# Second feed-forward of a two-layer block: hidden state kept transposed, mean square applied to the result

## The chip, the cores and the metric

The kernel runs on one core of a Trainium2 chip. The metric is the device time of one execution in microseconds (us), as a median over runs. One execution was also recorded by the hardware profiler; durations below come from it.

## What is computed

Two transformer layers over x, 2 sequences of 1024 rows of 256 numbers. Layer 0 is layer norm, causal attention (32 query heads, 8 key heads of 8) and beside it a GELU feed-forward in fp8. Layer 1 is layer norm, an attention among the 16 heads of 16 at each of the rows of a tile, and beside it the feed-forward that this change touches:

```
wq_gu = ternary_quant(w_gate_up)
gu = jnp.einsum('bsd,hd->bsh', x, wq_gu)
gate, up = jnp.split(gu, 2, axis=-1)
h = jax.nn.silu(gate) * up
hn = rms_norm(h)          # h / sqrt(mean(h*h) + eps), over the 1024 hidden units
wq_p = ternary_quant(w_proj)
return jnp.einsum('bsh,dh->bsd', hn, wq_p)
```

The result of each layer is added to x.

## The kernel before

The rows are cut in 16 tiles of 128. Every engine runs one fixed list of steps, the table `ORDER`: a step is a name and a number, `gu.63` or `qk.80`, and `run[name](n)` issues its instructions. The lists hold the steps of all stages of all tiles mixed; they set the order on each engine, and semaphores (`w.wait_ge`) hold a step back until its inputs and buffers are there. Nothing is reordered at run time between the matmuls of TensorE or on the other engines.

Layer 0's attention is 144 quads. A quad is four score matmuls (`qk`, L674) into the four banks `psS`, two exponentials on ScalarE (`exp`, L922) into `Pt`, and four f32 matmuls (`pv`, L688) into `psV`. All other matmuls fill the three shared PSUM banks `psM` (psA, psB, psC) in turn; a step may fill a bank only when the step three fills back has been read out.

The second feed-forward, tile n, with its steps:

- `xn1Tc` and `xl` make the normed tile, transposed (features on partitions), as a high and a low f16 part, `xhs`.
- `gu`, four steps a tile (TensorE, L837): `xhs` is the stationary operand, 512 columns of the ternary weights `wguT` stream. Four matmuls fill a bank with rows on partitions and 512 hidden units on the free axis.
- `tg` (ScalarE, tanh), `sg`, `hh` (VectorE): silu(gate) times up into `h1`, 128x1024 f32.
- `ssq` (ScalarE, L986): square with a running sum into `ss`; `ssm` (VectorE, L1402) and `rsg` (GpSimd, L1618) make 1/sqrt(mean + eps) of each row.
- `hxa` (ScalarE, L991) and `hx` (VectorE, L1408): `h1` times that factor, as a high and a low f16 part `hx_b`.
- `hxT`, two steps (TensorE, L847), eight transposes each; `hTc`, two steps (VectorE, L1416), copy them to SBUF as `hT`.
- `dn1` (TensorE, L856): 16 matmuls, `hT` stationary, 256 columns of `wpT` stream.
- `yo` adds the attention's result (from `at1T`, `wo1`), `yout` (VectorE, L1438) adds `dn1`'s, `ysum` sums absolute values for a check of range, and `out` stores the tile.

After the last tile a check (`rng`, `out_of_range`, L1444 to L1471) decides whether a second, safer pass has to run; it isn't run for these inputs. `h1`, `hx_b` and `hT` are single buffers, so `hh` of a tile waits for `hx` of the tile before it, and `hTc` for its `dn1`.

## Time and profile before

| what | value |
|---|---|
| median of 3 runs | 611.24 us (610.84 to 611.49) |
| the profiled execution, whole | 610.33 us |
| its span, first to last instruction | 608.6 us |
| mean granted TensorE clock | 0.988 |
| TensorE matmul busy | 559.7 us, 92% of the span |
| ScalarE busy | 468.5 us, 77% |
| VectorE busy | 445.6 us, 73% |
| GpSimd busy | 257.9 us, 42% |
| chain that ended last, by engine | PE 66%, DVE 13%, ACT 9%, issue 6%, DMA 2%, POOL 1% |

PE is TensorE, PEld its weight loads, DVE is VectorE, ACT ScalarE, POOL GpSimd. A matmul's recorded duration holds its way through the array, and consecutive ones overlap; what one costs the engine is the distance from its start to the start of the next. An f32 matmul with an f32 stationary operand is recorded as two.

### The profile page before, as it was taken

To read this page: it belongs to the slowest core of one execution; us is meant where nothing else is said; L and a number is where in the kernel's file an instruction comes from. 1 tells how busy PE (TensorE), PEld (TensorE's weight loads), DVE (VectorE), ACT (ScalarE), POOL (GpSimd) and SP (SyncE) were. 2 spreads that over 40 slices of the span, in tenths; PEclk is the share of its full clock that TensorE was granted. 3 is DMA by queue.
4 is the path that set the end of the run, shared out by engine and by line. 5 is a ranking of instruction groups with operands and counts; after the bars stand their busy time and mean duration, and the time that the engine had idled before them with its cause. 6 is when DMAs were issued, how large, how long until landed. Compare 5 with 4: busy or idle time off the path is not lost.

```text
span 608.6 us, 13144 instructions
## 1 busy us (share of the span) xinstructions
PE 559.7 (92%) x5040; PEld 290.9 (48%) x5085; DVE 445.6 (73%) x903; ACT 468.5 (77%) x605; POOL 257.9 (42%) x318
## 2 busy tenths in 40 slices
...
DMA packets 150915, 30.40 MB, mean 50 GB/s; under 512 B 133952, under 2 KB 149568, under 8 KB 150848
## 3 DMA queue, kind: packets, MB, share of 16 engines
...
q14 instruction: 26, 0.21, 0.1%
...
## 4 chain that ended last, share of the span: by engine, by line
PE 66%; DVE 13%; ACT 9%; issue 6%; DMA 2%; POOL 1%; SPq 0%; DVEq 0%; ACTq 0%; POOLq 0%
PE psV L688 16%; PE psS L674 7%; ACT Pt L922 5%; PE psA L837 3%; PE psS L791 3%; PE psC L837 2%; PE psB L837 2%; DMA stage<-in_wg 1%; PE psA L725 1%; PE psA L856 1%; PE psC L753 1%; PE psB L753 1%; PE psC L754 1%; DVE ga L1276 1%; DMA x<-in_x 1%
## 5 line engine op out<-in xcount | busy, mean ns | idle before, releaser
L922 ACT ACTIVATE Pt<-psS 128x1024 f32<-128x1024 f32 x288 | 280.5, 1036 | 45.7 <-PE psS L674 25.7
L688 PE MATMUL psV<-Pt,vaug 128*32 128x512 f32 x1152 | 147.1, 602 | 1.5 <-POOL Pt L1563 1.2
L1563 POOL TENSOR_SCALAR_AFFINE_SELECT Pt<-Pt 128x1024 f32<-128x1024 f32 x64 | 74.5, 1188 | 41.7 <-ACT Pt L922 41.5
L674 PE MATMUL psS<-qTf,kTf 32*128 32x512 f16 x576 | 72.4, 386 | 5.0 <-DVE qTf L1184 2.5
L674 PEld LDWEIGHTS psS<-qTf,kTf 32*128 32x128 f16 x576 | 19.5, 91 | 82.7 <-ACT Pt L922 45.1
L688 PEld LDWEIGHTS psV<-Pt,vaug 128*32 128x32 f32 x1152 | 26.1, 108 | 47.3 <-issue 37.6
L1618 POOL TENSOR_TENSOR ss<-ss,mhalf 128x1 f32<-128x1 f32 x16 | 9.8, 613 | 83.6 <-DVE ss L1402 83.5
L971 ACT ACTIVATE stage<-psS 128x1024 f32<-128x1024 f32 x32 | 31.1, 1025 | 12.5 <-PE psS L791 12.4
L1543 POOL TENSOR_TENSOR rt<-qkv,cs 128x320 f32<-128x320 f32 x16 | 17.0, 1059 | 50.0 <-DVE qkv L1138 47.1
L1554 POOL TENSOR_TENSOR QXf<-rt,QXf 128x512 f16<-128x512 f32 x16 | 21.4, 1339 | 35.3 <-ACT QXf L909 35.1
L1609 POOL TENSOR_TENSOR r<-qk,cos 128x256 f32<-128x256 f32 x16 | 13.0, 810 | 43.5 <-ACT qk L955 43.5
L1276 DVE SCALAR_TENSOR_TENSOR ga<-gw,gb 128x512 bf16<-128x512 f32 x32 | 29.1, 910 | 1.6 <-ACT gw L948 1.6
L1267 DVE SCALAR_TENSOR_TENSOR gw<-gw,gb 128x512 f32<-128x512 f32 x32 | 26.1, 815 | 1.7 <-ACT gw L937 1.7
L1408 DVE SCALAR_TENSOR_TENSOR qtmp<-qtmp,ss 128x1024 f16<-128x1024 f32 x16 | 21.5, 1345 | 5.8 <-ACT qtmp L991 5.7
L1599 POOL TENSOR_TENSOR xhs<-xn1T,xhs 128x256 f16<-128x256 f32 x16 | 12.2, 761 | 30.3 <-DVE xhs L1319 30.3
L1279 DVE TENSOR_TENSOR ga<-ga,fb 128x512 bf16<-128x512 bf16 x32 | 21.2, 663 | 3.7 <-ACT fb L943 0.5
L1546 POOL TENSOR_TENSOR rt<-qkv,sn 128x160 f32<-128x160 f32 x32 | 23.4, 751 | 0.0
L986 ACT ACTIVATE qtmp<-qtmp 128x1024 bf16<-128x1024 f32 x16 | 17.0, 1063 | 8.1 <-issue 5.1
L948 ACT ACTIVATE gw<-gw 128x512 f32<-128x512 f32 x32 | 20.8, 649 | 2.3 <-DVE gw L1267 2.2
L837 PE MATMUL psB<-wguT,xhs 128*128 128x512 bf16 x77 | 20.5, 379 | 2.0 <-issue 1.4
L837 PE MATMUL psA<-wguT,xhs 128*128 128x512 bf16 x75 | 19.8, 379 | 2.2 <-issue 1.0
L1283 DVE CAST a<-ga 128x512 fp8e4<-128x512 bf16 x32 | 20.9, 654 | 1.1
...
## 6 DMA issues: line engine op xcount, KB each, us to landing
...
```

The lines of the kernel that those rows point to most:

```text
L674: e.matmul(psS[j], kd[32 * j:32 * j + k, h, 128 * at:128 * at + 128], qd[32 * j:32 * j + k, 4 * h:4 * h + 4, :].rearrange("p s n -> p (s n ...
L688: ins = e.matmul(psV[32 * j:32 * j + 32, :], vaug[:, at, j, 32 * h:32 * h + 32], Pt[(4 * Q + j) % NP], start=(kb == 0 and h == 0), stop=(k ...
L837: ins = e.matmul(bank[:], src[:, pt, 128 * c:128 * c + 128], wguT[:, c, c0:c0 + 512], start=(k == 0), stop=(k == 3))
L922: e.activation(flat(Pt4[:, u % NP:u % NP + 2, :]), flat(psS4[:, j:j + 2, :]), ACT.Exp, scale=scale).then_inc(S["exp"], 1)
L971: e.activation(P1[:, 4 * b:4 * b + 8, :].rearrange("p g n -> p (g n)"), flat(psS4[:, b:b + 2, :]), ACT.Exp, scale=SC1).then_inc(S["ex1"], 1)
L1267: e.scalar_tensor_tensor(gw[:, half, :], gw[:, half, :], 1.0 / GA, gb[:, half, :], ALU.add, ALU.mult).then_inc(S["ge1"], 1)
L1276: e.scalar_tensor_tensor(a, gw[:, half, :], 1.0, gg, ALU.add, ALU.mult).then_inc(S["ge3"], 1)
L1279: e.tensor_tensor(a, a, fb[:, half, :], ALU.mult).then_inc(S["ge3"], 1)
L1408: e.scalar_tensor_tensor(hx_b[:, 1, :], h1, sn[:, 2:3], hx_b[:, 0, :], ALU.mult, ALU.subtract).then_inc(S["hx"], 1)
L1546: e.tensor_tensor(rb[:, :, :, ev], pairs[:, :, :, 1 - ev], snv[:, :, ev].unsqueeze(1).to_broadcast([128, 40, 4]), ALU.mult).then_inc(S["ro ...
L1554: e.tensor_tensor(X4[:, 0:32, 2:4, :], heads(rt[n % len(rt)][:, 0, 0:256], 2), X4[:, 0:32, 0:2, :], ALU.subtract).then_inc(S["ql"], 1)
L1563: e.affine_select(out=p, in_=p, pattern=[[0, 8], [1, 128]], compare_op=ALU.is_ge, fill=0.0, base=0, channel_multiplier=-1).then_inc(S["mas ...
```

## The change

The hidden state is made with hidden units on partitions. `gu` swaps its operands: 128 columns of the weights are stationary and the 128 columns of `xhs` stream, so that a bank holds four blocks of 128 hidden units by 128 rows. `h1` is then already what `dn1` needs as stationary operand, so `hxT` and `hTc` go. A row's sum of squares now lies across partitions: `ssq` writes the squares to `hsq`, `hsr` adds the eight blocks in one VectorE reduction (read with a stride of 128), and one more f32 matmul behind the 16 of `dn1`, against a column of ones, adds over the partitions into column 256 of the same bank. `msq` (VectorE) and `rsh` (GpSimd) make the factor, and `yout` multiplies `dn1`'s result with it. `hxa` and `hx` no longer wait for the factor. The check takes in the mean squares (`rngb`).

```diff
     "pe": (
-        "xnT.0 qkv.0 xnT.1 ts.0 ts.1 xnT.2 qkv.1 qxT.0 qxT.1 xnT.3 td.0 qk.0 td.1 tr.0 up.0 tr.1 qkv.2 qk.1 ts.2 "
...
+        "xnT.0 xnT.1 ts.0 ts.1 qkv.0 qkv.1 xnT.2 td.0 td.1 tr.0 qxT.0 tr.1 qxT.1 xnT.3 ts.2 qk.0 qk.1 qkv.2 pv.0 "
...
                 bank = shared("gu", m)
                 for k in range(4):
-                    c, pt = k % 2, k // 2
-                    c0 = 1024 * o + 512 * half
-                    ins = e.matmul(bank[:], src[:, pt, 128 * c:128 * c + 128], wguT[:, c, c0:c0 + 512], start=(k == 0),
-                                   stop=(k == 3))
+                    c0 = 1024 * o + 512 * half + 128 * k
+                    for i in range(4):
+                        c, pt = i % 2, i // 2
+                        ins = e.matmul(bank[:, 128 * k:128 * k + 128], wguT[:, c, c0:c0 + 128],
+                                       src[:, pt, 128 * c:128 * c + 128], start=(i == 0), stop=(i == 3))
                 ins.then_inc(S["gu"], 1)
-            def hxT(m):
...
-                for s in range(8):
-                    ins = e.transpose(bank[:, s, :], hx_b[:, pt, 128 * s:128 * s + 128], identh[:])
...
             def dn1(n):
-                w.wait_ge("hTc", 2 * n + 2)
+                w.wait_ge("hxa", n + 1)
+                w.wait_ge("hx", n + 1)
                 w.wait_ge("tw", 12)
                 bank = shared("dn1", n)
                 for k in range(16):
                     pt, s = divmod(k, 8)
-                    ins = e.matmul(bank[:, 0:256], hT[:, pt, s, :], wpT[:, s, :], start=(k == 0), stop=(k == 15))
+                    ins = e.matmul(bank[:, 0:256], hx_b[:, pt, 128 * s:128 * s + 128], wpT[:, s, :], start=(k == 0),
+                                   stop=(k == 15))
+                if n < NT:
+                    w.wait_ge("gz", 3)
+                    w.wait_ge("hsr", n + 1)
+                    ins = e.matmul(bank[:, 256:257], hsum, onesf[:, 0:1], start=True, stop=True)
                 ins.then_inc(S["dn1"], 1)
...
             def ssq(n):
                 w.wait_ge("hh", 2 * n + 2)
-                w.wait_ge("hxT", 2 * n)
-                w.wait_ge("hx", n)
-                e.activation(hx_b[:, 0, :].bitcast(BF16), h1, ACT.Square,
-                             accum_out=ss[n % len(ss)][:, 0:1]).then_inc(S["ssq"], 1)
+                w.wait_ge("hsr", n)
+                w.wait_ge("hnm", n - NT)
+                e.activation(hsq, h1, ACT.Square).then_inc(S["ssq"], 1)
 
             def hxa(n):
-                w.wait_ge("rsg", n + 1)
-                e.activation(hx_b[:, 0, :], h1, ACT.Copy, scale=ss[n % len(ss)][:, 2:3]).then_inc(S["hxa"], 1)
+                w.wait_ge("hh", 2 * n + 2)
+                w.wait_ge("hnm", n - NT + 1)
+                w.wait_ge("dn1", n)
+                e.activation(hx_b[:, 0, :], h1, ACT.Copy).then_inc(S["hxa"], 1)
...
+                w.wait_ge("ssq", n)
+                e.scalar_tensor_tensor(h1[:, 512 * half:512 * half + 512], sg1, 0.5 * UH if n < NT else 0.5, bank[:],
+                                       ALU.mult, ALU.mult).then_inc(S["hh"], 1)
...
+            def hsr(n):
+                w.wait_ge("sin", 1)
                 w.wait_ge("ssq", n + 1)
-                e.tensor_scalar(sn[:, 1:2], sn[:, 0:1], 1.0 / 1024, F32EPS, ALU.mult, ALU.add).then_inc(S["ssm"], 1)
+                w.wait_ge("dn1", n)
+                e.tensor_reduce(hsum, hsq.rearrange("p (s n) -> p n s", n=128), AX.X, ALU.add).then_inc(S["hsr"], 1)
...
             def hx(n):
-                sn = ss[n % len(ss)]
                 w.wait_ge("hxa", n + 1)
-                w.wait_ge("hxT", 2 * n)
-                e.scalar_tensor_tensor(hx_b[:, 1, :], h1, sn[:, 2:3], hx_b[:, 0, :], ALU.mult,
-                                       ALU.subtract).then_inc(S["hx"], 1)
-
-            def hTc(m):
-                n, pt = divmod(m, 2)
-                bank = psM[filled["hxT", m] % len(psM)][:].bitcast(F16).rearrange("p (s n) -> p s n", n=128)
-                w.wait_ge("hxT", m + 1)
                 w.wait_ge("dn1", n)
-                e.tensor_copy(hT[:, pt, :, :], bank).then_inc(S["hTc"], 1)
+                e.tensor_tensor(hx_b[:, 1, :], h1, hx_b[:, 0, :], ALU.subtract).then_inc(S["hx"], 1)
...
+            def msq(n):
+                bank = psM[filled["dn1", n] % len(psM)]
+                w.wait_ge("dn1", n + 1)
+                e.tensor_scalar(msqs[:, n:n + 1], bank[:, 256:257], 1.0 / 1024, F32EPS * UH * UH, ALU.mult,
+                                ALU.add).then_inc(S["msq"], 1)
...
+                if n < NT:
+                    w.wait_ge("rsh", n + 1)
+                    e.scalar_tensor_tensor(dst[:], bank[:, 0:256], ss[n % len(ss)][:], yo_b[n % len(yo_b)][:], ALU.mult,
+                                           ALU.add).then_inc(S["yout"], 1)
+                else:
+                    e.tensor_tensor(dst[:], bank[:, 0:256], yo_b[n % len(yo_b)][:], ALU.add).then_inc(S["yout"], 1)
...
+            def rsh(n):
+                w.wait_ge("msq", n + 1)
+                w.wait_ge("yout", n + 1 - len(ss))
+                e.tensor_tensor(ss[n % len(ss)][:], msqs[:, n:n + 1], mhalf[:], ALU.pow).then_inc(S["rsh"], 1)
```

All five lists of `ORDER` are written anew, in a different mix; TensorE's goes from 788 steps to 756, the 32 `hxT` fewer. Two places of them follow, as rows of instructions (line, operation, output<-streamed operand, stationary operand, size, count).

The first is TensorE's end of the program, before: from `dn1.13` (L856 into psB) over `gu.63` (L837) and the transposes of tile 14 (L847) to the first ones of tile 15.

```order
L856 MATMUL psB<-wpT,stmp 128x256 x16
L837 MATMUL psC<-wguT,xhs_1 128x512 x4
L847 MATMUL psA<-identh,qtmp 128x128 x8
L847 MATMUL psB<-identh,qtmp 128x128 x8
L579 MATMUL psC<-identf,at1_0 128x128
L580 MATMUL psC<-identf,at1_0 128x128
L823 MATMUL psA<-wo1,at1T_0 128x256
L824 MATMUL psA<-wo1,at1T_0 128x256
L856 MATMUL psB<-wpT,stmp 128x256 x16
L579 MATMUL psC<-identf,at1_0 128x128
L580 MATMUL psC<-identf,at1_0 128x128
L847 MATMUL psA<-identh,qtmp 128x128 x8
```

There follow `hxT.31`, `wo1.15` and `dn1.15`. The same engine in the change, from `gu.63` (now L843) to its last step but the check: L860 and L865 are `dn1` with its new last matmul, L828 and L829 `wo1`.

```order
L843 MATMUL psC<-xhs_1,wguT 128x128 x16
L860 MATMUL psA<-wpT,qtmp 128x256 x16
L865 MATMUL psA<-onesf,ang 128x1
L828 MATMUL psB<-wo1,at1T_0 128x256
L829 MATMUL psB<-wo1,at1T_0 128x256
L860 MATMUL psC<-wpT,qtmp 128x256 x16
L865 MATMUL psC<-onesf,ang 128x1
L584 MATMUL psA<-identf,at1_0 128x128
L585 MATMUL psA<-identf,at1_0 128x128
L828 MATMUL psB<-wo1,at1T_1 128x256
L829 MATMUL psB<-wo1,at1T_1 128x256
```

`gu.63` is 16 matmuls of 128 columns instead of 4 of 512, no transposes stand behind it, and the last attention tile (`at1T.15`, `wo1.15`) has moved behind `dn1.15`.

The second place is VectorE's end, before: `hh.31` (L1396), the copies of the transposes (L1416), `ssm.15` (L1402), `hx.15` (L1408).

```order
L1396 SCALAR_TENSOR_TENSOR qtmp<-stmp,psC 128x512
L1416 COPY stmp<-psA 128x1024
L1422 COPY at1T_0<-psC 128x256
L1402 TENSOR_SCALAR ss_1<-ss_1 128x1
L1416 COPY stmp<-psB 128x1024
L1428 TENSOR_TENSOR yo_0<-psA,x 128x256
L1408 SCALAR_TENSOR_TENSOR qtmp<-qtmp,ss_1 128x1024
L1422 COPY at1T_1<-psC 128x256
L1438 TENSOR_TENSOR yout_0<-psB,yo_0 128x256
L1441 TENSOR_REDUCE ysum<-yout_0 128x1
L1416 COPY stmp<-psA 128x1024
```

In the change, from `msq.14` (L1446) on: `hx` is L1429, `hsr` L1414, `yout` L1459, `rngb` L1486 to L1491; the operations of `rng` now stand ahead of this piece.

```order
L1446 TENSOR_SCALAR msqs<-psA 128x1
L1429 TENSOR_TENSOR qtmp<-qtmp 128x1024
L1441 TENSOR_TENSOR yo_0<-psB,x 128x256
L1414 TENSOR_REDUCE ang<-stmp 128x128
L1459 SCALAR_TENSOR_TENSOR yout_0<-psA,ss_0,yo_0 128x256
L1465 TENSOR_REDUCE ysum<-yout_0 128x1
L1446 TENSOR_SCALAR msqs<-psC 128x1
L1435 COPY at1T_1<-psA 128x256
L1486 TENSOR_SCALAR hq<-msqs 128x16
L1488 SCALAR_TENSOR_TENSOR hq<-msqs,hq 128x16
L1491 TENSOR_REDUCE hl<-hq 128x1
L1441 TENSOR_TENSOR yo_1<-psB,x 128x256
```

The copies are gone, `hsr.15` stands behind `hx.15`, and `msq` stands between `dn1` and `yout`.

## Rows read from the trace of the kernel before

**Rows 1.** The page's first part: busy us, share of the span, instructions

```profile
PE 559.7 (92%) x5040; PEld 290.9 (48%) x5085; DVE 445.6 (73%) x903; ACT 468.5 (77%) x605; POOL 257.9 (42%) x318
```

**Rows 2.** Windows: length, busy of each engine (count), PEclk, DMA share, GB/s

```profile
60.00:100.00 40.00, 35.87 (x280) 15.87 (x282) 36.33 (x74) 39.21 (x53) 26.64 (x30) 1.00 0.08 27
...
350.00:500.00 150.00, 147.68 (x1403) 75.86 (x1410) 92.21 (x191) 120.87 (x150) 52.48 (x65) 1.00 0.21 36
545.00:590.00 45.00, 43.18 (x477) 30.32 (x475) 34.26 (x71) 18.82 (x25) 6.70 (x10) 1.00 0.55 88
```

**Rows 3.** Timeline of TensorE at `hxT`: start, length, operation

```profile
477.69 0.61 PE L847 MATMUL psB<-identh,qtmp 128*128 128x128 f16 x8
478.23 1.07 PE L688 MATMUL psV<-Pt,vaug 128*32 128x512 f32 x8
...
577.54 0.61 PE L847 MATMUL psB<-identh,qtmp 128*128 128x128 f16 x8
577.98 0.61 PE L847 MATMUL psC<-identh,qtmp 128*128 128x128 f16 x8
578.43 0.61 PE L758 MATMUL psA<-identf,w8g 128*128 128x128 f32 x4
```

**Rows 4.** The instructions of L847: ns min/median/max, first and last start

```profile
L847 PEld LDWEIGHTS psB<-identh,qtmp x120: 95/98/99, 139.2 to 596.9; 128*128 128x128 f16 x120
```

**Rows 5.** Timeline of TensorE at `gu`

```profile
568.79 1.03 PE L837 MATMUL psB<-wguT,xhs 128*128 128x512 bf16 x4
569.65 1.03 PE L837 MATMUL psC<-wguT,xhs 128*128 128x512 bf16 x3
```

**Rows 6.** Timeline of TensorE, small f32 steps: two transposes, then `wo1`

```profile
532.74 0.27 PE L580 MATMUL psC<-identf,xn 128*128 128x128 f32 x1
532.85 0.60 PE L758 MATMUL psA<-identf,w8g 128*128 128x128 f32 x4
...
585.26 0.70 PE L823 MATMUL psB<-wo,at1T 128*128 128x256 f32 x2
585.80 0.59 PE L824 MATMUL psB<-wo,at1T 128*128 128x256 f32 x2
```

**Rows 7.** Groups by form, ScalarE and VectorE: busy us, mean ns, idle before

```profile
L991 ACT ACTIVATE qtmp<-qtmp,ss 128x1024 f16<-128x1024 f32 x16 | 18.5, 1159 | 1.9 <-POOL ss L1618 1.7
L986 ACT ACTIVATE qtmp<-qtmp 128x1024 bf16<-128x1024 f32 x16 | 17.0, 1063 | 8.1 <-issue 5.1 <-PE psB L847 3.0
L986 ACT ACTIVATION_READ_ACCUMULATOR qtmp<-qtmp 128x1 f32 x16 | 3.3, 203 | 0.0
L1408 DVE SCALAR_TENSOR_TENSOR qtmp<-qtmp,ss 128x1024 f16<-128x1024 f32 x16 | 21.5, 1345 | 5.8 <-ACT qtmp L991 5.7
L1416 DVE COPY stmp<-psB 128x1024 f16<-128x1024 f16 x15 | 10.3, 684 | 3.4 <-PE psB L847 3.4
L1450 DVE TENSOR_REDUCE hl<-rec 128x1 f32<-128x512 f32 x1 | 0.7, 675 | 0.0
L1451 DVE TENSOR_REDUCE hl<-rec 128x1 f32<-128x256 f32 x1 | 0.4, 410 | 0.0
```

**Rows 8.** Timeline of the end: `dn1.13`, `gu.63`, then VectorE's `yout.15` and the flag

```profile
587.53 1.91 PE L856 MATMUL psB<-wpT,stmp 128*128 128x256 bf16 x16
589.49 0.81 PE L837 MATMUL psC<-wguT,xhs 128*128 128x512 bf16 x3
590.14 0.61 PE L847 MATMUL psA<-identh,qtmp 128*128 128x128 f16 x8
...
601.00 0.42 DVE L1438 TENSOR_TENSOR yout<-psA,yo 128x256 f32<-128x256 f32 x1
...
603.02 0.14 DVE L1471 TENSOR_SCALAR flag<-hl 1x1 int32<-1x1 f32 x1
```

**Rows 9.** Instructions of `ssm` (ns min/median/max), then the group of the `pow`

```profile
L1402 DVE TENSOR_SCALAR ss<-ss x16: 121/144/155, 130.0 to 592.5; 128x1 f32<-128x1 f32 x16
...
L1618 POOL TENSOR_TENSOR ss<-ss,mhalf 128x1 f32<-128x1 f32 x16 | 9.8, 613 | 83.6 <-DVE ss L1402 83.5
```

More of the change, by code:

```diff
@@ L31 @@
 MAGIC = 12582912.0
+UH = 1024.0
+HLOW, HHIGH = 1.0, 3.9e6
 TWO_PI = 2.0 * np.pi
@@ L187 @@
     "pe": "xnT qkv qxT:0 qxT:1 QUADS up:0 up:1 up:2 up:3 down obT attT wo0 xn1T qkv1:0 qkv1:1 "
[3 rows of a table removed]
[2 rows of a table added]
     "dve": "ln0 xn xnTc qkvc va wide q0 kl kTc qTc ob ge1:0 ge3:0 ge1:1 ge3:1 yff att attTc "
[3 rows of a table removed]
[3 rows of a table added]
     "sp": "vw vr ow at1r out",
 }
[L197 removed]
+PARTS = {"qxT": 2, "fxT": 3, "fTc": 3, "mT": 2, "up": 4, "qkv1": 2, "gT": 2, "gu": 4, "sq": 2, "fh": 2, "th": 2,
          "tg": 2, "mTc": 2, "g": 2, "ge1": 2, "ge3": 2, "sg": 2,
[L199 removed]
+         "hh": 2, "ge4": 2}
 ROUND2 = {e: r.replace("qxT:0 qxT:1", "fxT:0 fxT:1 fxT:2 rmm mT:0 mT:1").replace(" kl kTc qTc", " fTc:0 fTc:1 fTc:2 rmax mTc:0 mTc:1")
[L202 removed]
+          .replace(" ql", "").replace("gu:3", "gu:3 hsb").replace("hxa ssq", "ssq hxa").replace("hsr", "hsr hib hnm")
+          .replace(" msq", "").replace("rsh", "rsb") for e, r in ROUND.items()}
 QUAD_STAGES = {"pe": ("qk", "pv"), "act": ("exp",), "pool": ("mask",)}
@@ L241 @@
     "o1T": lambda n: ("o1", 2 * n + 2), "at1T": lambda n: ("at1Tc", n + 1), "wo1": lambda n: ("yo", n + 1),
-    "gu": lambda m: ("hh" if m % 2 else "sg", m // 2 + 1), "hxT": lambda m: ("hTc", m + 1), "dn1": lambda n: ("yout", n + 1),
+    "gu": lambda m: ("hh" if m % 2 else "sg", m // 2 + 1), "hsb": lambda n: ("hib", n - NT + 1), "dn1": lambda n: ("yout", n + 1),
     "ts": lambda m: ("tsc", m + 1), "td": lambda m: ("tde", m + 1), "tr": lambda m: ("tw", m + 1),
```

80 lines of the change are left out of this document (45 added, 35 removed), and 268 rows, old and new, of tables (ORDER, ROUND).

## The prediction

> **What bounds the kernel now.** I began with the busy shares [rows 1]. TensorE is at 92% of a span of 608.6 us, ScalarE at 77%, VectorE at 73%. A share over the whole span can hide stages, so the windows came next [rows 2]. From 60 to 100 us three engines are nearly full: TensorE 35.87 of 40, ScalarE 39.21, VectorE 36.33. From 350 to 500 us TensorE is busy 147.68 of 150 us, while ScalarE has 29 us free and VectorE 58. From 545 to 590 us, behind the last quad, it is still 43.18 of 45. So from about 100 us on the time is the sum of what TensorE is given to do, plus small waits. All steps of the second feed-forward lie there: the first `hxT` starts at 139.2 us [rows 4]. Work that is taken from TensorE after 100 us comes off the time nearly one for one, until one of the others fills up; work that is taken from ScalarE or VectorE is worth little.
>
> What a step costs TensorE is read from start to start, not from the durations, which overlap. Eight transposes of `hxT` take 577.98 - 577.54 = 0.44 us, 0.45 in the next one, and 0.54 where an f32 step follows [rows 3]. Four matmuls of `gu` take 0.86 us [rows 5].
>
> **`hxT` goes.** 32 steps at 0.44 to 0.54 us are 14.1 to 17.3 us of TensorE; I take 0.47, so -15.0 us.
>
> **`gu` in narrow matmuls.** Streamed columns stay the same, 2048 a step; loads of stationary operands go from 4 to 16. The nearest row is `hxT` itself: f16 operands, 128 columns streamed over 128 loaded, each with a load of its own. Its 16 matmuls in two steps take 578.43 - 577.54 = 0.89 us [rows 3], so the load of 98 ns [rows 4] is mostly hidden behind the matmul before it, at 56 ns a pair. A `gu` step then costs 0.89 instead of 0.86. What a narrow last matmul no longer covers is the load of the next step: the step of 0.54 against 0.44 shows up to 0.1 us. I take +0.05 us for each of 64 steps, so +3.2 us; the ends are +0.03 (1.9 us) and +0.13 (8.3 us).
>
> Of the loads the Trainium skill says otherwise: "TensorE: Matmul & The Clock Gate", section "Back-to-back issue gap", gives a sustained 81 ns a matmul at 128 columns and 131 ns at 512, where each has a load of its own. By it a `gu` step would go from 4 x 131 = 0.52 to 16 x 81 = 1.30 us, and the 64 steps would cost 50 us more, an estimate from that page. This trace disagrees at both sizes: 56 ns and 215 ns [rows 3, 5].
>
> **One more matmul in `dn1`.** It is f32, so two records, each with an f32 load of 128 columns, and it streams one column. Nothing like it stands in the trace. From below, an f32 transpose of 128 columns takes 0.11 us [rows 6]; from above, an f32 matmul of 256 columns ahead of another takes 0.54 us [rows 6]. Two loads that nothing covers put it in the middle: 0.3 us, 16 times, +4.8 us (1.8 to 8.6).
>
> **TensorE's sum** is -15.0 + 3.2 + 4.8 = -7.0 us, the ends -17.3 + 1.9 + 1.8 = -13.6 and -14.1 + 8.3 + 8.6 = +2.8.
>
> **ScalarE.** `ssq` no longer reads its sum out, -0.20 us, and `hxa` is a plain copy with no factor, about 0.1 us less than its 1159 ns [rows 7]: -0.3 us a tile, 4.8 in all, none of it on the path while TensorE leads. If TensorE does fall by 7 us, ScalarE stays 80 us below it.
>
> **VectorE.** Two copies go, -1.37 us a tile [rows 7], and `ssm`, 0.14 [rows 9]. `hx` keeps its 1024 elements and two inputs; I leave it at 1.35. `hsr` is a reduction over 1024 f32. The two of 512 and 256 take 675 and 410 ns [rows 7], so 265 ns for 256 elements more, and 675 + 530 = 1.2 us for 1024. They read neighbours, `hsr` reads with a stride; twice the time, 2.3 us, is my other end. `msq`, as small as `ssm`, adds 0.14, `yout`'s factor nothing. So VectorE changes by -0.2 to +0.9 us a tile, covered by its free 58 of 150 us. The `pow` keeps its 613 ns [rows 9], on an engine at 42%.
>
> **Waits.** Before, a tile went `hh`, `ssq`, `ssm`, `rsg`, `hxa`, `hx`, `hxT`, `hTc`, `dn1`. Now it goes `hh`, `hxa`, `hx`, `dn1`: shorter by 1.06 + 0.20 + 0.14 + 0.61 in front and 0.45 + 0.68 behind [rows 3, 7, 9], over 3 us. While quads are left this latency was covered by them. Behind the last quad TensorE idles 45 - 43.18 = 1.8 us up to 590 us, and I take 0.5 of it for this latency: -0.5 us (0 to -1.8).
>
> **The end.** Before, `gu.63` ends at 590.14 and the flag at 603.16: 13.0 us [rows 8]. In the change, from the end of `gu.63` (T): `dn1.14` stands right behind it, 16 matmuls of about 0.11 us [rows 8] and the new one, and ends T+2.1; `hxa.15` has to wait for it, since `hx_b` is single, and ends T+3.3; `hx.15` T+4.7. `yo.14` and `hsr.15` on VectorE end T+6.3, within the 1.8 us of `dn1.15`'s 16 matmuls; `dn1.15` ends T+6.9. Then `at1T.15`, its copy and `wo1.15` (0.2 + 0.6 + 1.0, the last from rows 6), `yo` and `yout`, which starts at T+9.3; `msq` and `rsh`, 0.14 + 0.61, run beside them. From the start of `yout` to the flag it was 603.16 - 601.00 = 2.2 us [rows 8], so T+11.5: 1.5 us shorter. That is the four steps of `hxT` that stood behind `gu.63`, less the new matmuls, and both are in TensorE's sum. Its idle time there stays as it was, so the end adds nothing.
>
> **Sum.** 610.33 us (the profiled execution, 608.6 of it span) - 7.0 - 0.5 = 602.8. The median of the runs was 0.9 us above that execution, so 603.7, and I write 603.5.
>
> **Rivals.** (a) *Waits take it back.* The lists are mixed anew, and `hsr`, `hxa` and `ssq` hang on `dn1` of the tile before through single buffers, `hh` on both `ssq` and `hx`. For it speaks that three engines are nearly full at 60 to 100 us [rows 2], where more work put ahead gains nothing; against it, that TensorE's list is the shorter one behind 100 us, and waits in the long middle are 2.3 us in 150. All 7.5 us back: 611.2. Chance 0.06.
>
> (b) *Slower: `dn1` stands for `hsr`.* The last matmul of `dn1` waits at the head of TensorE's list for VectorE's reduction, and the quads' `qk` and `pv` behind it wait too, and after them ScalarE. In 13 of 16 tiles `hsr` stands behind `hx` in VectorE's list, with one to some 25 steps between. The gain is gone when that wait reaches 7.5 / 16 = 0.47 us a tile. With `hsr` at 2.3 us and a step of 0.7 us ahead of it, against a cover of 1.8 us by the 16 matmuls, it is 2.3 + 0.7 - 1.8 = 1.2 us a tile: 603.5 + 19 = 623. Against it: outside the last tiles other steps of TensorE stand between `hx` and `dn1`. Chance 0.07.
>
> (c) *Slower: loads set the pace of `gu`.* If a matmul of 128 columns can't hide its load there, a pair costs the 98 ns of the load [rows 4], a step 1.57 instead of 0.91 us, 64 of them +42: 646. The page of the Trainium skill above has a rule of this kind. `hxT` in rows 3 speaks against it with the same shapes and types of 16 bits. Chance 0.02.
>
> **How the numbers follow.** The likeliest case, TensorE's sum, has 0.85 and 599.5 to 608.5 as its own range: half the way from -7.0 to each end of the sum (3.3 and 4.9 us), since the ends don't fall together. The full range reaches from 598.5 (latency worth 1.5 us more than I took) to 610.5, which takes in the near part of (a), and leaves out (b) and (c). About 0.2%, 1.2 us, is what a measurement of this kernel can tell. Of the likeliest case nearly all lies below 610.0: faster 0.84. Same is (a) and the upper edge, 0.06. Slower is (b), (c) and a rest of 0.01: 0.10.
>
> **What would show it.** TensorE busy near 552 us and the rest of the span unchanged; 0.89 to 0.99 us from start to start of a `gu` step; 0.1 to 0.5 us for the lone f32 matmul, and no idle time ahead of it that ends at `hsr`; `hsr` near 1.2 us. The forecast is wrong if the `gu` steps show 1.1 us or more, if TensorE's busy share falls below 90% between 100 and 545 us (then waits took the gain), or if the quads before 100 us come so much later that the rest can't catch up.

## The result: 616.5 us, slower by 0.9%

The changed kernel takes 616.47 us (median of 4 runs, 616.01 to 618.03), the kernel before beside it 611.04 (4 runs, 610.79 to 611.49): a ratio of 1.0093, 95% interval 1.0074 to 1.0112, or 5.4 us. The forecast was 603.5 us with a range of 598.5 to 610.5. The profiled execution took 616.43 us, 614.6 of it span, at a mean granted clock of 0.980.

The page of the changed kernel, its first part (of before in [rows 1]) and the chain that ended last, by engine:

```profile
PE 561.7 (91%) x5619; PEld 316.4 (51%) x5629; DVE 457.1 (74%) x889; ACT 466.4 (76%) x589; POOL 261.3 (43%) x319
...
PE 58%; DVE 21%; issue 8%; ACT 7%; POOL 3%; DMA 1%; another core or an unknown queue 0%; DVEq 0%; SPq 0%; ACTq 0%; POOLq 0%
```

VectorE has 11.5 us more to do, inside the -3.2 to +14.4 us that the forecast gave it (-0.2 to +0.9 us a tile), and its share of the last chain has gone from 13% to 21%, TensorE's from 66% to 58%. TensorE's 561.7 us can't be set against the 559.7 of before: the trace of before lacks records of it (38 of the 256 matmuls of `gu` among them). Its steps are compared from start to start below.

Two windows of the changed kernel, columns as in [rows 2]:

```profile
60.00:100.00 40.00, 34.15 (x269) 15.75 (x264) 36.73 (x70) 30.80 (x44) 27.16 (x33) 0.96 0.04 14
...
350.00:500.00 150.00, 147.58 (x1542) 81.16 (x1542) 95.36 (x184) 122.01 (x145) 59.51 (x71) 1.00 0.25 40
```

The long middle looks as before: 147.58 of 150 us against 147.68. The first window doesn't. From 60 to 100 us ScalarE works 30.80 us where it worked 39.21, TensorE 34.15 where it worked 35.87, and VectorE is as full as it was, 36.73 against 36.33 [rows 2].

**Where the time went.** Two fixed places in the program cut the span in three: the scores of quad 20 (`qk.20`), and the step behind `gu.63`. Their rows in the timeline of TensorE, first before (the second place is in [rows 8]), then the change:

```profile
100.41 0.40 PE L674 MATMUL psS<-qTf,kTf 32*128 32x512 f16 x4
```

```profile
114.37 0.40 PE L679 MATMUL psS<-qTf,kTf 32*128 32x512 f16 x4
...
596.41 1.06 PE L843 MATMUL psC<-xhs,wguT 128*128 128x128 f16 x16
597.30 1.91 PE L860 MATMUL psA<-wpT,qtmp 128*128 128x256 bf16 x16
```

The step behind `gu.63` starts at 590.14 us before [rows 8] and at 597.30 now. So:

| stretch of the span, us | before | change | difference |
|---|---|---|---|
| start to `qk.20` | 100.4 | 114.4 | +14.0 |
| `qk.20` to the step behind `gu.63` | 489.7 | 482.9 | -6.8 |
| from there to the end | 18.5 | 17.3 | -1.2 |
| span | 608.6 | 614.6 | +6.0 |

Behind `qk.20` the change gains 8.0 us, about what was forecast (7.5). The 14.0 us lost ahead of it, for which the sum had no term, make the whole slower. ScalarE's exponentials, two for each quad, show the same, and no record of them is missing. The windows of that line alone (ScalarE's busy time and count), before:

```profile
0.00:100.00 100.00, 39.33 (x40) 0.95 0.31 107
0.00:150.00 150.00, 63.25 (x65) 0.97 0.25 80
```

and in the change:

```profile
0.00:100.00 100.00, 32.12 (x33) 0.91 0.33 107
0.00:150.00 150.00, 55.38 (x57) 0.94 0.26 80
```

Seven exponentials of 40 are missing at 100 us, eight of 65 at 150.

**The new and changed steps.** `gu` and `dn1` in the changed kernel's timeline of TensorE:

```profile
560.25 1.91 PE L860 MATMUL psA<-wpT,qtmp 128*128 128x256 bf16 x16
562.00 0.28 PE L865 MATMUL psA<-onesf,ang 128*128 128x1 f32 x2
562.14 0.68 PE L828 MATMUL psB<-wo,at1T 128*128 128x256 f32 x2
...
564.29 1.07 PE L843 MATMUL psC<-xhs,wguT 128*128 128x128 f16 x16
565.19 1.00 PE L843 MATMUL psA<-xhs,wguT 128*128 128x128 f16 x15
```

A `gu` step takes 565.19 - 564.29 = 0.90 us, as forecast from `hxT` (0.89); the loads are hidden. `dn1`'s last matmul takes 562.14 - 562.00 = 0.14 us here, the whole `dn1` 1.89. That is so where the next step's stationary operand is 128x128; in front of smaller ones, as in `qk` and `pv`, it mostly takes 0.21, and over the 16 tiles it comes to 3.3 us. Groups of the page, columns as in [rows 7]:

```profile
L1414 DVE TENSOR_REDUCE ang<-stmp 128x128 f32<-128x1024 f32 x16 | 31.3, 1958 | 0.0
...
L1001 ACT ACTIVATE qtmp<-qtmp 128x1024 f16<-128x1024 f32 x16 | 17.1, 1068 | 14.0 <-PE psA L865 7.7
```

`hsr` (L1414) takes 1958 ns and not 1200: 31.3 us of VectorE in all. `hxa` (L1001) has 14.0 us of waiting in front of it that were 1.9 before [rows 7]: it fills the single `hx_b`, so it stands until `dn1` of the tile before has read it. The wait that VectorE has in front of `msq`, from the table of waits (us in total, times, longest):

```profile
DVE msqs L1446 <- PE psA L865: 12.1, 4, 5.0
```

`dn1` fills three banks in turn; with the other two (3.5 and 2.3) VectorE stands 17.9 us in front of `msq` until `dn1` is there. Rival (b), `dn1`'s last matmul standing at the head of TensorE's list until `hsr` is done, costs hardly anything: the matmul L865 waits for `ang` (the sum that `hsr` writes) twice, 0.7 us in total.

### The profile page after: what moved, and what is told of

The parts are those of the page before. It is cut to its first block, busy times and chain, and to the rows that moved or that the text cites. A ratio compares the mean times of both kernels' runs of the same rounds, so it can differ in the third digit from the quotient of the medians.

```text
span 614.6 us, 14254 instructions
## 1 busy us (share of the span) xinstructions
PE 561.7 (91%) x5619; PEld 316.4 (51%) x5629; DVE 457.1 (74%) x889; ACT 466.4 (76%) x589; POOL 261.3 (43%) x319
## 4 chain that ended last, share of the span: by engine, by line
PE 58%; DVE 21%; issue 8%; ACT 7%; POOL 3%; DMA 1%; another core or an unknown queue 0%; DVEq 0%; SPq 0%; ACTq 0%; POOLq 0%
PE psV L693 15%; PE psS L679 7%; ACT Pt L931 5%; PE psA L843 2%; PE psS L796 2%; DVE ga L1286 2%; PE psB L843 2%; PE psC L843 2%; DVE ga L1289 2%; PE psB L758 1%; DVE ang L1414 1%; PE psB L759 1%; PE psA L860 1%; DMA x<-in_x 1%; PE psC L730 1%
## 5 line engine op out<-in xcount | busy, mean ns | idle before, releaser
L931 ACT ACTIVATE Pt<-psS 128x1024 f32<-128x1024 f32 x288 | 279.4, 1028 | 48.2 <-PE psS L679 31.6
L1649 POOL TENSOR_TENSOR ss<-msqs,mhalf 128x1 f32<-128x1 f32 x16 | 11.0, 685 | 96.4 <-DVE msqs L1446 96.4
L1414 DVE TENSOR_REDUCE ang<-stmp 128x128 f32<-128x1024 f32 x16 | 31.3, 1958 | 0.0
L1286 DVE SCALAR_TENSOR_TENSOR ga<-gw,gb 128x512 bf16<-128x512 f32 x32 | 26.0, 814 | 2.6 <-ACT gw L957 2.5
L1001 ACT ACTIVATE qtmp<-qtmp 128x1024 f16<-128x1024 f32 x16 | 17.1, 1068 | 14.0 <-PE psA L865 7.7
L1641 POOL TENSOR_TENSOR r<-qk,cos 128x256 f32<-128x256 f32 x16 | 13.6, 850 | 31.3 <-ACT qk L964 31.3
L1558 POOL TENSOR_SCALAR rs<-mv 128x1 f32<-128x1 f32 x16 | 5.2, 326 | 51.0 <-DVE mv L1123 51.0
L843 PE MATMUL psA<-xhs,wguT 128*128 128x128 f16 x384 | 25.5, 219 | 1.2 <-DVE x L1272 1.2
L843 PEld LDWEIGHTS psA<-xhs,wguT 128*128 128x128 bf16 x384 | 22.2, 98 | 7.5 <-issue 6.1
L1429 DVE TENSOR_TENSOR qtmp<-qtmp 128x1024 f16<-128x1024 f32 x16 | 20.2, 1261 | 4.0 <-ACT qtmp L1001 4.0
L843 PEld LDWEIGHTS psB<-xhs,wguT 128*128 128x128 bf16 x336 | 19.4, 98 | 6.3 <-issue 4.0
L843 PE MATMUL psB<-xhs,wguT 128*128 128x128 f16 x336 | 22.3, 219 | 0.3 <-DVE qtmp L1407 0.2
```

The costliest lines, as they stand in the source:

```text
L843: ins = e.matmul(bank[:, 128 * k:128 * k + 128], wguT[:, c, c0:c0 + 128], src[:, pt, 128 * c:128 * c + 128], start=(i == 0), stop=(i == 3))
L931: e.activation(flat(Pt4[:, u % NP:u % NP + 2, :]), flat(psS4[:, j:j + 2, :]), ACT.Exp, scale=scale).then_inc(S["exp"], 1)
L1286: e.scalar_tensor_tensor(a, gw[:, half, :], 1.0, gg, ALU.add, ALU.mult).then_inc(S["ge3"], 1)
L1414: e.tensor_reduce(hsum, hsq.rearrange("p (s n) -> p n s", n=128), AX.X, ALU.add).then_inc(S["hsr"], 1)
```

## The experiments

All times below are medians on the chip beside runs of the kernel before on the same chip (610.96 to 611.11 us). "The change" is the changed kernel, 616.5. Its four runs spread over 2 us, so a difference from it of under 1.5 us is no more than noise. Of an edit to the lists only the first line of TensorE's is shown. Two theories were open at first: the lists of the start cost the time (L), or the new work on VectorE and TensorE does (W).

**Narrow `gu` alone**, in the kernel before:

```diff
-                    c0 = 1024 * o + 512 * half
-                    ins = e.matmul(bank[:], src[:, pt, 128 * c:128 * c + 128], wguT[:, c, c0:c0 + 512], start=(k == 0),
-                                   stop=(k == 3))
+                    c0 = 1024 * o + 512 * half + 128 * k
+                    for i in range(4):
+                        c, pt = i % 2, i // 2
+                        ins = e.matmul(bank[:, 128 * k:128 * k + 128], src[:, pt, 128 * c:128 * c + 128],
+                                       wguT[:, c, c0:c0 + 128], start=(i == 0), stop=(i == 3))
```

> The kernel before with one edit: a gu step is 16 matmuls of 128 streamed columns instead of 4 of 512, operands not swapped, lists unchanged. If the narrow form is nearly free (the prediction: +0.05 us a step, 64 steps) the time is 611.0 + 3.2 = 614.2, range 612.5 to 616. The trace of the change shows 0.98 us from the start of a gu step to the next start, against 0.91 before, which gives +4.5. If loads set the pace, +42 us, 653.

Measured 612.86 us (611.82 to 613.44), ratio 1.0034 (1.0021 to 1.0046): +1.9 us, the lower end of the forecast's 1.9 to 8.3. Rival (c), loads that set the pace (646 us), is out.

**The new start in the old kernel.**

```diff
-        "xnT.0 qkv.0 xnT.1 ts.0 ts.1 xnT.2 qkv.1 qxT.0 qxT.1 xnT.3 td.0 qk.0 td.1 tr.0 up.0 tr.1 qkv.2 qk.1 ts.2 "
+        "xnT.0 xnT.1 ts.0 ts.1 qkv.0 qkv.1 xnT.2 td.0 td.1 tr.0 qxT.0 tr.1 qxT.1 xnT.3 ts.2 qk.0 qk.1 qkv.2 pv.0 "
```

> The kernel before, computing as before, but each engine's list begins with the steps that the change had started by 118 us of its trace (up to about quad 20), in the change's order, and goes on with the old list less those steps. Theory L (the new order of the first 100 us is what costs): quads 20 to 30 come 8 to 10 us late and the loss stays, 617 to 620 us. Theory W (the new work of the feed-forward costs, the start is paid back): 610 to 612 us.

Measured 621.8 us (621.29 to 622.22), ratio 1.0187 (1.0170 to 1.0204): +10.8 us, from the lists alone, with every instruction as before. That is theory L, and 1.8 us above its range. Its timeline:

```profile
113.14 0.39 PE L677 MATMUL psS<-qTf,kTf 32*128 32x512 f16 x4
...
600.50 0.81 PE L840 MATMUL psC<-wguT,xhs 128*128 128x512 bf16 x3
601.15 0.61 PE L850 MATMUL psA<-identh,qtmp 128*128 128x128 f16 x8
```

`qk.20` starts at 113.1 us, 12.7 later than before and 1.2 ahead of the change. Behind it the old kernel's 489.7 us become 488.0: of what was done early, 1.7 us are paid back. From 60 to 100 us this run has ScalarE at 32.37 us busy and VectorE at 36.86. Its granted clock up to 150 us is 0.97, the same as before, so the loss at the start isn't the clock's; the change has 0.94 there.

**Squares written so that `hsr` reads neighbours**, in the change:

```diff
-                e.activation(hsq, h1, ACT.Square).then_inc(S["ssq"], 1)
+                e.activation(hsq.rearrange("p (n s) -> p s n", s=8), h1.rearrange("p (s n) -> p s n", n=128),
+                             ACT.Square).then_inc(S["ssq"], 1)
...
-                e.tensor_reduce(hsum, hsq.rearrange("p (s n) -> p n s", n=128), AX.X, ALU.add).then_inc(S["hsr"], 1)
+                e.tensor_reduce(hsum, hsq.rearrange("p (n s) -> p n s", s=8), AX.X, ALU.add).then_inc(S["hsr"], 1)
```

> The change, with ScalarE writing the squares so that the eight of one sum lie side by side, and VectorE's reduction reading neighbours. If the stride of 512 bytes is what made hsr 1.96 us, it falls to about 1.2 us. Theory W: 12 us less on VectorE, 2 to 5 us less in all, 611.5 to 614.5. Theory L: 616 as the change. If ScalarE's scattered write is slow, ssq rises above 1.06 us and takes it back.

Measured 619.42 us (618.5 to 621.28), ratio 1.0156 (1.0135 to 1.0177): 2.9 us more than the change. Groups of this kernel, `ssq` and `hsr`:

```profile
L995 ACT ACTIVATE stmp<-qtmp 128x1024 f32<-128x1024 f32 x16 | 33.5, 2093 | 2.9 <-DVE qtmp L1408 2.8
...
L1415 DVE TENSOR_REDUCE ang<-stmp 128x128 f32<-128x1024 f32 x16 | 19.4, 1210 | 0.4 <-ACT stmp L995 0.4
```

Over neighbours the reduction takes 1210 ns, what the forecast had worked out from [rows 7]. The stride adds 750 ns. But ScalarE's scattered write costs 2093 ns where the plain one took 1059, and 16.5 us more of ScalarE outweigh 12.0 less of VectorE.

**A short reduction.** Only the first of the eight blocks is added; the other seven are left out.

```diff
-                e.tensor_reduce(hsum, hsq.rearrange("p (s n) -> p n s", n=128), AX.X, ALU.add).then_inc(S["hsr"], 1)
+                e.tensor_reduce(hsum, hsq[:, 0:128].rearrange("p (s n) -> p n s", n=128), AX.X,
+                                ALU.add).then_inc(S["hsr"], 1)
```

> The change, with hsr adding only the first of the eight blocks (seven are left out of the sum), about 0.25 us instead of 1.96: prices the reduction by itself. Theory W: 27 us less on VectorE, 5 us or more off the time, 608 to 612. Theory L: less than 1 us, 615.5 to 616.5.

Measured 611.54 us (610.22 to 614.81, 10 runs), ratio 1.0009 (0.9994 to 1.0025). The reduction takes 277 ns, 26.9 us less of VectorE in all, and the time falls by 4.9: 0.18 us for each us. So the new work costs as well (W), beside the lists.

**The old start in the change** (the steps started by 110 us are those of the change, in the order of before):

```diff
-        "xnT.0 xnT.1 ts.0 ts.1 qkv.0 qkv.1 xnT.2 td.0 td.1 tr.0 qxT.0 tr.1 qxT.1 xnT.3 ts.2 qk.0 qk.1 qkv.2 pv.0 "
+        "xnT.0 qkv.0 xnT.1 ts.0 ts.1 xnT.2 qkv.1 qxT.0 qxT.1 xnT.3 td.0 qk.0 td.1 tr.0 up.0 tr.1 qkv.2 ts.2 qk.1 "
```

> The change; of each list, the steps that start before 110 us of its trace are the same steps, but among themselves in the order that the lists before have; behind them nothing is moved. Theory L (the new order of the first 100 us costs about 11 us, as the run with the new start showed on the old program): 606 to 609 us, quad 20 at 100 to 106 us instead of 114. Theory W (the new work costs): 615 to 617.

Measured 614.75 us (613.4 to 615.77), ratio 1.0064 (1.0041 to 1.0087): 1.7 us less than the change, little more than noise, and far from the 606 to 609 of theory L. `qk.15` starts at 84.3 us, as before (83.8), but `qk.20` at 111.0. The order within the start hardly matters: where the same set of steps has to be done by 110 us, the quads behind it come late.

**The old start and the short reduction together.** The edits are those of the two above.

> The same, and hsr adds only the first of eight blocks (seven are left out). If the order of the start and the reduction are the two costs and they add: 616.5 - 9 - 5 = 602, which would be the gain of the prediction. If the reduction only costs because VectorE is behind after the bad start: the same time as with the old start alone, 606 to 609.

Measured 610.49 us (609.13 to 613.57, 10 runs), ratio 0.9993 (0.9976 to 1.0011): 1.05 us under the short reduction alone, where the old start alone had given 1.7. Both are near the noise.

**Without the seventeenth matmul.** The sum over the partitions is left out, and `msq` reads a constant in its place.

```diff
-                if n < NT:
-                    w.wait_ge("gz", 3)
-                    w.wait_ge("hsr", n + 1)
-                    ins = e.matmul(bank[:, 256:257], hsum, onesf[:, 0:1], start=True, stop=True)
```

> The change without the 17th matmul of dn1, and without its wait for hsr; the factor comes from a constant (the sum over partitions is left out, hsr still runs). The prediction's price is 0.3 us a tile, 4.8 us: 611.7. By the trace of the change, dn1 with it takes 0.2 us more than 16 matmuls: 613. If TensorE also stood for hsr there, more than 5 us come off: under 611.

Measured 614.91 us (613.62 to 616.32), ratio 1.0063 (1.0039 to 1.0086): it and its wait cost 1.6 us, little more than noise, where the forecast had 4.8.

**Other lists for the kernel before**, found by a search over a model of the steps' durations:

```diff
-        "xnT.0 qkv.0 xnT.1 ts.0 ts.1 xnT.2 qkv.1 qxT.0 qxT.1 xnT.3 td.0 qk.0 td.1 tr.0 up.0 tr.1 qkv.2 qk.1 ts.2 "
+        "xnT.0 qkv.0 ts.0 xnT.1 xnT.2 ts.1 qkv.1 qxT.0 qxT.1 td.0 td.1 qk.0 xnT.3 up.0 tr.0 tr.1 qkv.2 qk.1 ts.2 "
```

> The kernel before, with lists found by a search over many small moves of steps; nothing else changed. If the lists are worth as much as the 11 us of the new start say, good lists can be faster than the given ones by some us: 595 to 608. If the given ones are near the best for this program: 611 or more.

Measured 613.12 us (610.74 to 614.06), ratio 1.0036 (1.0022 to 1.0050). No gain: the lists of before are not easily improved, and not every new mix costs as much as the change's does. This one puts 118 steps of TensorE's list ahead of `qk.20`, where before has 117 and the change 127, and starts it at 102.3 us.

At this point two terms were found, and the assumption under the whole forecast was still untried: that behind 100 us TensorE's work counts one for one and VectorE's not at all. The next three put a price on each, all in the kernel before.

**Every transpose of `hxT` twice.**

```diff
-                for s in range(8):
+                for s in [*range(8), *range(8)]:
```

> The kernel before, in which each of the 32 hxT steps does its eight transposes twice into the same bank: 32 x 0.45 = 14.4 us more of TensorE, nothing else. If the time from 100 us on is the sum of TensorE's steps, as the prediction said, it comes out one for one: 611.0 + 14.4 = 625.4 us (623.5 to 627). If latencies and the other engines share the bound, a part is absorbed in TensorE's waits: under 621 us, and then taking the same steps away gives less than their 16 us as well.

Measured 621.34 us (620.53 to 622.07), ratio 1.0174 (1.0157 to 1.0191). The timeline shows the doubled step at 0.90 us:

```profile
473.37 1.07 PE L847 MATMUL psC<-identh,qtmp 128*128 128x128 f16 x16
474.27 0.28 PE L579 MATMUL psA<-identf,att 128*128 128x128 f32 x1
```

So 14.4 us of TensorE's work (32 steps longer by 0.45) cost 10.2 us, 0.71 for each us, between the two expectations: not one for one.

**A reduction more on VectorE, ahead of `hx`.**

```diff
+                e.tensor_reduce(yjunk[:], h1.rearrange("p (s n) -> p n s", n=128), AX.X, ALU.add)
                 e.scalar_tensor_tensor(hx_b[:, 1, :], h1, sn[:, 2:3], hx_b[:, 0, :], ALU.mult,
```

> The kernel before, with a reduction of the shape and stride of hsr (1.96 us) ahead of each hx on VectorE, whose result nobody reads: 16 x 1.96 = 31.3 us more of VectorE, at the place where the change has hsr or near it. The shortened reduction gave 5 us for 27 us of VectorE's work, 0.19 each. If VectorE's work costs that at any place: 611.0 + 6 = 617 us. If VectorE's free time in the long middle covers it, as the prediction said: 611 to 612 us. If the chain hh, ssq, hxa, hx is what TensorE waits for, more than in the change: 620 us or over.

Measured 631.4 us (631.07 to 631.74), ratio 1.0337 (1.0319 to 1.0354): +20.3 us for 31.3 us of VectorE's work, 0.65 for each us. The group and the window of the long middle:

```profile
L1409 DVE TENSOR_REDUCE yjunk<-qtmp 128x128 f32<-128x1024 f32 x16 | 31.3, 1958 | 5.8 <-ACT qtmp L992 5.7
...
350.00:500.00 150.00, 144.02 (x1336) 73.22 (x1332) 95.93 (x195) 117.59 (x146) 50.85 (x65) 1.00 0.25 41
```

TensorE is idle for 6.0 of 150 us instead of 2.3, and ScalarE has got through 3.3 us less. VectorE is busy for only 96 of 150 us all the while.

**The same reduction behind `hx`.**

```diff
                                        ALU.subtract).then_inc(S["hx"], 1)
+                e.tensor_reduce(yjunk[:], flat(wqkv1[:])[:, 0:1024].rearrange("p (s n) -> p n s", n=128), AX.X, ALU.add)
```

> The kernel before, with a reduction of the shape and stride of hsr (1.96 us, over weights that never change, result unused) directly behind each hx on VectorE instead of ahead of it. The chain hh, ssq, ssm, hxa, hx, hxT keeps its length; VectorE has the same 31.3 us more to do. If VectorE's work costs by its amount, as much as TensorE's: again near 631 us. If the 20 us of the one ahead were the longer chain: under 620 us. A split between them tells how much each is.

Measured 629.3 us (628.23 to 630.25), ratio 1.0308 (1.0289 to 1.0327): +18.3 us for 31.0 us, 0.59 for each us. Behind the chain from `hh` to `hx` the work costs nearly as much as in it. What it makes late is whatever stands next in VectorE's list: `hh` of a coming tile in 6 of 16 cases, the copies `hTc` of this one 2 to 24 steps on. Which of these the time goes to isn't shown.

**Three sums in place of the strided reduction**, in the change:

```diff
-                e.tensor_reduce(hsum, hsq.rearrange("p (s n) -> p n s", n=128), AX.X, ALU.add).then_inc(S["hsr"], 1)
+                e.tensor_tensor(hsq[:, 0:512], hsq[:, 0:512], hsq[:, 512:1024], ALU.add).then_inc(S["hst"], 1)
+                e.tensor_tensor(hsq[:, 0:256], hsq[:, 0:256], hsq[:, 256:512], ALU.add).then_inc(S["hst"], 1)
+                e.tensor_tensor(hsum, hsq[:, 0:128], hsq[:, 128:256], ALU.add).then_inc(S["hsr"], 1)
```

> The change, with hsr as three additions of neighbours (512, 256 and 128 columns of f32) in place of one strided reduction of 1024; the result is the same sum. By rows of the change at about 1 ns a column and 0.1 us of overhead, the three take 0.6 + 0.35 + 0.2 = 1.2 us for 1.96 us, so 12 us less of VectorE. At 0.19 us a us: 616.5 - 2.3 = 614.2 us. If what costs is only that hsr is long at some places of VectorE's list, up to the 5 us of the shortened one: 611.5. If three instructions that wait for each other take as long as one: 616.5.

Measured 615.21 us (614.33 to 616.46), ratio 1.0072 (1.0051 to 1.0093). The three groups:

```profile
L1414 DVE TENSOR_TENSOR stmp<-stmp 128x512 f32<-128x512 f32 x16 | 11.2, 697 | 0.0
...
L1416 DVE TENSOR_TENSOR stmp<-stmp 128x256 f32<-128x256 f32 x16 | 8.3, 522 | 0.6
...
L1418 DVE TENSOR_TENSOR ang<-stmp 128x128 f32<-128x128 f32 x16 | 5.4, 340 | 0.5
```

Together 1559 ns, not the 1200 of the expectation: 6.4 us less of VectorE and 1.3 us less time. That would be 0.20 for each us, but 1.3 us is within the noise of two such medians.

**The squares summed on TensorE**, in the change; `ssq` writes bf16 into two buffers, so it waits for the `dn1` two tiles back and no longer for `hsr`, which is gone from the list:

```diff
-                    w.wait_ge("hsr", n + 1)
-                    ins = e.matmul(bank[:, 256:257], hsum, onesf[:, 0:1], start=True, stop=True)
+                    w.wait_ge("ssq", n + 1)
+                    for s in range(8):
+                        ins = e.matmul(bank[:, 256:257], hsq16[:, n % 2, 128 * s:128 * s + 128], ones16, start=(s == 0),
+                                       stop=(s == 7))
```

> The change, with ScalarE's squares written as bf16 in two buffers and summed on TensorE: dn1 ends with eight matmuls of one column over the eight blocks of squares in place of the one f32 matmul, and hsr goes from VectorE (31.3 us less). TensorE: 8 x 56 ns = 0.45 us for about 0.17, so +4.5 us in all, at the measured 0.7 a us +3.2. VectorE: the shortened reduction gave 5.0 us for 27 us, so -5.8 for all of it. Sum: 616.5 + 3.2 - 5.8 = 614 us. If VectorE's work at this place costs what it did ahead of hx in the kernel before (0.65 a us): 616.5 + 3.2 - 20 = 600 us. If the loads of 98 ns set the pace of one-column matmuls: 0.78 us a tile, 617 us.

Measured 612.0 us (611.29 to 613.55, 10 runs), ratio 1.0016 (1.0003 to 1.0028): 4.5 us less than the change. `dn1` in its timeline:

```profile
557.23 1.91 PE L862 MATMUL psA<-wpT,qtmp 128*128 128x256 bf16 x16
558.98 0.34 PE L868 MATMUL psA<-onesf,stmp 128*128 128x1 bf16 x8
559.18 0.68 PE L830 MATMUL psB<-wo,at1T 128*128 128x256 f32 x2
```

Eight matmuls of one column, each with a load of its own, take 559.18 - 558.98 = 0.20 us, so the whole `dn1` is 1.95 us against 1.89 with the one f32 matmul. 31.3 us of VectorE's work are bought with 1 us of TensorE's. What the second buffer of the squares gives by itself, the run doesn't tell.

**The start of before in the change.** In head_of_before the set of steps started by 70 us is that of the kernel before as well, and the steps up to 200 us are put anew to fit. Three waits come in with it, by which the copies `vr`, `ow` and `at1r` to and from memory wait for the one before of their kind; the next two kernels have them too. Their own price wasn't measured.

The first line of the list:

```diff
-        "xnT.0 xnT.1 ts.0 ts.1 qkv.0 qkv.1 xnT.2 td.0 td.1 tr.0 qxT.0 tr.1 qxT.1 xnT.3 ts.2 qk.0 qk.1 qkv.2 pv.0 "
+        "xnT.0 qkv.0 xnT.1 ts.0 ts.1 xnT.2 qkv.1 qxT.0 qxT.1 xnT.3 td.0 qk.0 td.1 tr.0 up.0 tr.1 qkv.2 qk.1 ts.2 "
```

> The change, all its own steps and costs, but the lists start with the set of steps that the kernel before had started by 70 us, in its order; the steps behind it up to about 200 us are put in a new order to fit. If the change's start of the lists is what costs it 9 to 11 us: 605 to 609 us. If the loss is only pushed behind the spliced part, as when the first 110 us were taken over: 613 to 616 us. If the new order behind the splice is worse than the one it replaces: over 617 us, and the run tells nothing on the start.

Measured 611.9 us (611.27 to 613.55, 10 runs), ratio 1.0019 (1.0007 to 1.0030): 4.6 us less than the change, between the first two expectations. `qk.10` starts at 65.0 us instead of 76.1, but `qk.20` at 115.6: the delay is moved from ahead of quad 10 to behind it, and `qk.50` is 3.0 us earlier than in the change. So the loss at the start isn't in its first 70 us as such.

**That start, with the three sums** (head_tree, the edit of tree_sum).

> The kernel with the start of the lists as before (611.9 us), and with hsr as three additions of neighbours, which gave 1.3 us in the change. Separate costs: 610.6 us, within 0.2% of the kernel before. The same cost seen twice: 611.9.

Measured 612.31 us (611.26 to 614.68, 10 runs), ratio 1.0029 (1.0014 to 1.0044). No gain over the kernel it is made from; the expected 1.3 us are about what two such medians can differ by, so this run decides nothing.

**That start, with the squares summed on TensorE** (the edit of squares_on_pe).

> The kernel with the start of the lists as before (611.9 us), and with the squares summed on TensorE as in squares_on_pe. If the two costs are separate, its difference from head_of_before is that of squares_on_pe from the change: 611.9 - 2.6 = 609.3 us, just faster than the kernel before. If they are the same queue on VectorE seen twice: 611 to 612 us.

Measured 607.15 us (606.28 to 608.1), ratio 0.9939 (0.9918 to 0.9961): 3.8 us faster than the kernel before, 9.3 than the change. Its page, first part, and its timeline of TensorE:

```profile
PE 558.0 (92%) x5716; PEld 315.8 (52%) x5725; DVE 421.5 (70%) x873; ACT 465.9 (77%) x589; POOL 263.0 (43%) x319
```

```profile
113.55 0.39 PE L686 MATMUL psS<-qTf,kTf 32*128 32x512 f16 x4
...
587.73 1.06 PE L850 MATMUL psC<-xhs,wguT 128*128 128x128 f16 x16
588.62 1.91 PE L867 MATMUL psA<-wpT,qtmp 128*128 128x256 bf16 x16
```

VectorE is busy 35.6 us less than in the change. `qk.20` is still 13.1 us late, but from there to the step behind `gu.63` it takes 475.1 us where before took 489.7. The two gains add up: 4.6 + 4.5 = 9.1, measured 9.3, where the expectation had 609.3 us at best.

## Why the prediction was wrong

**The step that failed** is in the prediction's first part: "from about 100 us on the time is the sum of what TensorE is given to do", and with it the sum, which has no term for the lists. That the engines are nearly full at the start was read correctly from [rows 2], and rival (a) said that more work put ahead gains nothing there. It should have asked what it costs. All of the lists were new, and no row of before shows how a new mix runs. With the old instructions in the new lists the start loses 12.7 us at `qk.20` and 10.8 in the time, which is measured (new_start). The last line of the prediction names it as what would make it wrong, quads before 100 us that come too late; it was given no price and no chance of its own.

What delays the quads there is narrowed down, not settled. The windows from the start to `qk.20`, first before, then new_start, columns as in [rows 2]:

```profile
0.00:100.41 100.41, 74.14 (x540) 32.50 (x547) 87.03 (x169) 74.26 (x100) 62.73 (x80) 0.95 0.31 107
```

```profile
0.00:113.14 113.14, 82.52 (x578) 36.37 (x588) 96.59 (x190) 78.54 (x107) 69.17 (x88) 0.95 0.28 95
```

By then VectorE has worked 9.6 us more, in 21 more instructions, and TensorE 8.4 us more: the new lists put more work of later tiles ahead of quad 20. The kernels agree with this. Ahead of `qk.20` TensorE's list has 117 steps before and 118 in before_searched, which start it at 100.4 and 102.3 us; the kernels with 127 and 131 steps (the change, new_start, old_start and those with the start of before) start it at 111.0 to 115.6. VectorE is nearly full all the while (86.6 and 85.4 of the first 100 us, before and in the change), so what is put ahead in its list most likely puts the quads back, and ScalarE then waits: 8.7 us less of its work is done by 100 us. The order within the set explains little of it (old_start, 1.7 us), the first 70 us alone don't (head_of_before), and the clock doesn't. Why only 1.7 us of the work done early come back later is open, and no run took single steps out of the start.

**"Work that is taken from ScalarE or VectorE is worth little"** fell too. VectorE's work added to the kernel before costs 0.59 to 0.65 us for each us, TensorE's 0.71. A free 58 of 150 us don't cover it. The likely reason, which no run isolates, is that the list is taken in order: what VectorE has free is time in which it stands in front of a step that isn't ready, such as the 17.9 us before `msq` in the change. Within the change, leaving out most of `hsr`'s work gave only 0.18 for each us, and moving it to TensorE 4.5 us for 31.3. So work taken away in one kernel was worth a third of work added in the other. Why was not found: no run adds VectorE's work to the change or takes it from the kernel before, so whether the kernels differ or adding and removing do isn't shown.

**`hsr` at 1.2 us** was sized by rows that read neighbours; it takes 1.96. The other end, 2.3 us, held it. The term missing was its price in time: the 26.9 us that the short one leaves out are worth 4.9 us, and summing on TensorE 4.5.

**TensorE's sum** of -7.0 was too small a gain. From start to start and without idle time, the 32 steps of `hxT` took 15.7 us (forecast 15.0). The 64 of `gu` rose by 1.9 us, from 59.0 (in longer_hx, whose trace has every matmul of them) to 60.9 (forecast 3.2), and `dn1` with its new matmul by 2.5, from 29.1 to 31.6 (forecast 4.8). Together -11.3 us, at 0.71 each -8.0. VectorE's +11.5 us at 0.2 add 2.3. That gives -5.7, an estimate, for all but the lists. Behind `qk.20` the change measured -8.0, of which the lists' early work, by new_start, is -1.8 (1.7 in the middle, 0.1 at the end): -6.2. So the forecast 7.5 us for this part came out nearly right, by two errors that cancel: a gain too small, and all of it counted. No run separates the edits here from the lists behind 118 us, which are new in the change too, so that the 6.2 us are the edits' alone is argued, not shown.

The prediction's own range for its likeliest case doesn't follow from its terms either: half the way to the ends, 3.3 and 4.9 us, gives 600.2 to 608.4 and not 599.5 to 608.5.

**The shorter chain** (-0.5 us) was priced by no run. `hxa` stood 12.1 us more than before in front of the single `hx_b`, a wait that rival (a) named and the chain's sum left out.

**The end** came out nearly as worked: `dn1.15` at T+7.1 (forecast 6.9), `yout` starting at T+9.7 (9.3), the flag at T+12.0 (11.5), with T = 597.30.

**The rivals.** (a) had the right place and the wrong depth: at worst it took back all 7.5 us, to 611.2. The sign for waits behind 100 us, TensorE under 90% busy from 100 to 545 us, didn't show: it was busy 434.8 of 445 us. (b) did not happen as a wait of `dn1` for `hsr` (0.7 us in all). (c) did not happen: 0.90 us a `gu` step. The Trainium skill's "TensorE: Matmul & The Clock Gate", section "Back-to-back issue gap", would have had 1.30; the trace of the changed kernel disagrees with it as that of before did.

**The sum with the measured terms:** -6.2 behind `qk.20` by the edits and whatever the later lists do, +10.8 by the lists of the start, gives 4.6 us; the time measured 5.4. The change reaches `qk.20` another 1.2 us later than new_start does, which is more than the 0.8 left over. Its granted clock was lower there (0.94 against 0.97); that this is the reason isn't shown. The sum is the timeline's own accounts, so that it closes proves no cause.
